# A two-stage recurrence on one core: three engines loop over 64 steps instead of 8, one gate semaphore is split by parity, and VectorE makes its next wait value at another place

## What is computed

```python
# stage 1, GRU over keys: x = keys @ Wx + b, then for each of 1024 steps
z = sigmoid(xz + (h @ Wh)_z);  r = sigmoid(xr + (h @ Wh)_r)
h = z * h + (1 - z) * relu(xh + r * (h @ Wh)_h)        # all h are kept as outs
# between: attn = softmax over time of outs . (queries @ W_att.T)
# stage 2, attention GRU over outs, 1024 steps more
r = sigmoid(xr + (h @ Wh)_r);  c = relu(xc + r * (h @ Wh)_c)
h = (1 - a) * h + a * c                                 # a = attn[b, t]
```

## Time and profile before

| | |
|---|---|
| median of 3 runs | 4424.12 us (4422.9 to 4429.71) |
| profiled execution | 4430.53 us |
| its span, first to last instruction | 4428.7 us |
| granted TensorE clock, mean | 0.997 |
| GRU loops | about 16 to 2316 us |
| attention loops | about 2353 to 4425 us |

### The profile page before, as it was taken

The page is one execution under the profiler, slowest core; times in us unless marked ns, Lnnn a source line. Parts: engine busy times, 40 slices in busy tenths (PEclk is TensorE's granted clock), DMA queues, the critical chain, the costliest instruction groups (busy, mean ns, idle before and its releaser), DMA issues.

```text
span 4428.7 us, 336421 instructions
## 1 busy us (share of the span) xinstructions
PE 4372.4 (99%) x131196; PEld 3968.0 (90%) x131196; DVE 4196.2 (95%) x24625; ACT 2286.8 (52%) x9363; POOL 2717.1 (61%) x6154
## 2 busy tenths in 40 slices
PE   8999999999999999999998999999999999999999
PEld 7888888888888888888887999999999999999998
DVE  8999999999999999999998999999999999999999
ACT  5666666666666666666654444444444444444444
POOL 6777777777777777777773444444444444444444
PEclk9999999999999999999998999999999999999999
DMA  3333333333333333334334555555555555554554
GB/s 110 115 116 123 115 116 123 115 115 121 117 115 120 119 115 120 119 115 121 118 123 129 129 132 128 128 132 128 128 133 128 128 133 128 128 133 129 127 133 115
DMA packets 169275, 544.13 MB, mean 123 GB/s; under 512 B 31644, under 2 KB 38060, under 8 KB 169260
## 3 DMA queue, kind: packets, MB, share of 16 engines
q1 hardware_dynamic: 169260, 543.93, 44.3%
HBM read 405.24 MB, written 138.56 MB: 123 GB/s over the span
## 4 chain that ended last, share of the span: by engine, by line
DVE 52%; PE 21%; issue 20%; DMA 3%; DVEq 2%; SPq 1%; ACT 0%; ACTq 0%; PEldq 0%
DVE vec_bank L525 12%; DVE gated L448 8%; DVE state L538 7%; DVE a_new L532 6%; DVE vec_bank L455 5%; DVE gated L519 5%; DVE vec_bank L464 5%; DVE h L475 4%; PE r_bank_a L561 4%; PE r_bank_b L561 3%; DMA logits<-logit_rows 2%; PE logit_bank L623 2%; PE z_bank_b L569 2%; PE z_bank_a L569 2%; PE c_bank_a L561 1%
## 5 line engine op out<-in xcount | busy, mean ns | idle before, releaser
L331 POOL TENSOR_TENSOR a_kept<-attn_rest,state 128x128 f32<-128x128 f32 x2048 | 933.6, 456 | 1173.6 <-DVE state L538 1139.0
L314 POOL TENSOR_TENSOR kept<-z_gate,h 128x128 f32<-128x128 f32 x2048 | 933.6, 456 | 533.8 <-ACT z_gate L360 512.0
L304 POOL TENSOR_TENSOR prod<-h,qw 128x128 f32<-128x128 f32 x2050 | 934.6, 456 | 0.0
L569 PE MATMUL r_bank_a<-x,weights 64*64 64x128 f32 x8200 | 881.7, 290 | 12.8 <-ACT r_gate L389 7.1
L569 PE MATMUL r_bank_b<-x,weights 64*64 64x128 f32 x8192 | 892.8, 295 | 0.0
L569 PE MATMUL z_bank_a<-x,weights 64*64 64x128 f32 x8200 | 853.9, 283 | 0.0
L569 PE MATMUL z_bank_b<-x,weights 64*64 64x128 f32 x8192 | 843.3, 283 | 0.0
L623 PE MATMUL logit_bank<-prod,row_sum 64*64 64x128 f32 x8208 | 798.5, 270 | 8.6 <-ACT logit_rows L349 5.0
L464 DVE SCALAR_TENSOR_TENSOR vec_bank<-vec_bank,z_rest 128x64 f32<-128x64 f32 x4096 | 735.9, 225 | 0.4 <-issue 0.3
L475 DVE TENSOR_TENSOR h<-vec_bank,kept 128x64 f32<-128x64 f32 x4096 | 721.3, 218 | 0.0
L389 ACT ACTIVATE r_gate<-r_bank_a 128x128 f32<-128x128 f32 x1024 | 284.0, 277 | 837.5 <-PE r_bank_a L561 837.5
(11 more groups left out here) (119 smaller groups left out, 17857.4 us busy)
## 6 DMA issues: line engine op xcount, KB each, us to landing
x<-in_keys_t SPq DMA_DIRECT2D x512, 256.0 KB, 3.7
gru_outputs<-h SPq DMA_DIRECT2D x256, 512.0 KB, 2.9
x<-gru_outputs SPq DMA_DIRECT2D x512, 256.0 KB, 3.7
attn<-attention SPq DMA_DIRECT2D x512, 256.0 KB, 3.9
logits<-logit_rows SPq DMA_DIRECT2D x258, 8.0 KB
time_rows<-logits SPq DMA_DIRECT2D x2, 896.0 KB, 7.0
attention<-time_rows SPq DMA_DIRECT2D x2, 896.0 KB, 5.5
weights<-in_weight_columns SPq DMA_DIRECT2D x2, 176.0 KB, 3.7
```

The lines of the kernel that those rows point to most:

```text
L304: nc.gpsimd.tensor_tensor(prod[:, (s - 1) % BODY, gcols(g)], h_at(s - 1)[:, gcols(g)], qw[:, gcols(g)], ALU.mult).then_inc(prod_ready[g], 1)
L314: nc.gpsimd.tensor_tensor(kept[:, g], z_gate[:, g], h_at(s - 1)[:, gcols(g)], ALU.mult).then_inc(kept_ready[g], 1)
L331: nc.gpsimd.tensor_tensor(a_kept[:, s % 2, gcols(g)], attn_rest[:, s % 2, gcols(g)], state[:, (s - 1) % 2, gcols(g)], ALU.mult).then_inc(a ...
L569: last = nc.tensor.matmul(dst[lanes(half)], weights[lanes(1 - half), w], moving[lanes(1 - half)], start=start, stop=False, skip_group_chec ...
```

## The change

VectorE, ScalarE and GpSimd loop over bodies of `SPAN = 64` written-out steps; TensorE and SP keep bodies of 8. `r_ready` and `ar_ready` become two semaphores each, for even and odd steps, off which TensorE takes 4 at the last two steps of its body; with them go the wait and the increment at a body's start. VectorE's `due` no longer is an expression but a register, filled one step ahead, behind the second group's candidate. Values that depended on `s` within 8 steps are taken `s % BODY`.

```diff
+SPAN = 8 * BODY
-        r_ready, z_ready, zr_ready = sems("r_ready"), sems("z_ready"), sems("z_rest_ready")
+        r_ready, ar_ready, anew_ready = parity_sems("r_ready"), parity_sems("ar_ready"), parity_sems("anew_ready")
+        def by_parity(s):
+            return s % BODY // 2 + 1
...
-            with act.Fori(0, T, BODY) as t0:       # the same on pool and dve, in both stages
-                for s in range(BODY):
-                    if s == 2:
-                        copy_logits(t0)
+            with act.Fori(0, T, SPAN) as t0:
+                for s in range(SPAN):
+                    if s % BODY == 2:
+                        copy_logits(t0 + (s - 2))
...
             def gru_gated(due, s, g):
-                if s == 0:
-                    dve.wait_ge(r_summed[g], due)
-                    dve.sem_inc(bodies_begun, 1)
                 dve.wait_ge(rh_summed[g], due)
-                dve.wait_ge(r_ready[g], s + 2)
+                dve.wait_ge(r_ready[g][s % 2], by_parity(s))
...
-                stored = t0 * ONES + 16
-                for s in range(BODY):
-                    due = t0 + (s + 2)
+                soon = count(0, t0, 2)              # reg_add into one of two registers
+                for s in range(SPAN):
+                    due = soon
+                    if s % CHUNK == 0:
+                        stored = t0 * ONES + 16 * (s // BODY + 1)
                     for g in GROUPS:
                         gru_gated(due, s, g)
                         gru_cand(due, s, g)
+                        if g == 1:
+                            soon = count(s + 1, t0, s + 3)
                         gru_new(due, s, g)
                         gru_h(due, stored, s, g)
...
             def agru_gated(due, s, g):
-                if s == 0:
-                    dve.wait_ge(ar_summed[g], due)
-                    dve.sem_inc(bodies_begun, 1)
-                dve.wait_ge(ar_ready[g], s + 2)
+                dve.wait_ge(ar_ready[g][s % 2], by_parity(s))
                 dve.wait_ge(rc_summed[g], due)
...
                     agru_cand(due, s, 1)
+                    soon = count(s + 1, t0, s + 3)
                     agru_new(due, pairs, s, 1)
...
-                        pe.wait_ge(r_ready[o], seen_by_pe(s, o))
+                        pe.wait_ge(r_ready[o][(n - 1) % 2], by_parity(n - 1))
-                        if n % BODY == 0:
-                            last.then_inc(ar_ready[o], -BODY)
+                        if (n - 1) % BODY >= BODY - 2:
+                            last.then_inc(ar_ready[o][(n - 1) % 2], -HALF)
```

More of the change, by code:

```diff
@@ L26, in recurrent_attention_kernel @@
     BM = HALVES * COLS // P
-    assert HALVES == 2 and GC == P and T % BODY == 0
+    assert HALVES == 2 and GC == P and T % SPAN == 0
     BODIES = T // BODY
@@ L56, in part_sems, with parity_sems @@
             return [[sem(f"{name}_{'ab'[g]}{part}") for part, _ in PARTS] for g in GROUPS]
+        def parity_sems(name):
+            return [[sem(f"{name}_{'ab'[g]}_{('even', 'odd')[parity]}") for parity in range(2)] for g in GROUPS]
         weights = sb("weights", [P, 11, U])
@@ L305, in product @@
                                         ALU.mult).then_inc(prod_ready[g], 1)
-            with pool.Fori(0, T, BODY) as t0:
-                for s in range(BODY):
+            with pool.Fori(0, T, SPAN) as t0:
+                for s in range(SPAN):
                     due = t0 + (s + 2)
@@ L338, in _ @@
                 act.sem_inc(zr_ready[g], FIRST)
-                for q in (r_ready[g], ar_ready[g]):
-                    act.sem_inc(q, (1, FIRST)[g])
+            act.sem_inc(r_ready[1][1], HALF)
+            act.sem_inc(ar_ready[1][1], HALF)
             act.sem_inc(rest_ready, 1)
@@ L349, in copy_logits @@
                 nc.scalar.activation(logit_rows[:], logit_bank[:, 0:COLS], ACT.Copy).then_inc(logits_copied, BODY)
-            with act.Fori(0, T, BODY) as t0:
-                for s in range(BODY):
-                    if s == 2:
-                        copy_logits(t0)
+            with act.Fori(0, T, SPAN) as t0:
+                for s in range(SPAN):
+                    if s % BODY == 2:
+                        copy_logits(t0 + (s - 2))
                     due = t0 + (s + 2)
@@ L460, in gru_new @@
                 for part, c in PARTS:
-                    dve.wait_ge(cand_ready[g][part], (due, s + 2)[part])
+                    dve.wait_ge(cand_ready[g][part], (due, s % BODY + 2)[part])
                     if part == 0:
-                        dve.wait_ge(zr_ready[g], s + 2)
+                        dve.wait_ge(zr_ready[g], s % BODY + 2)
                     nc.vector.scalar_tensor_tensor(new[:, c], cand[:, c], 0.0, z_rest[:, g, c],
@@ L473, in gru_h, with count @@
                         if g == 0 and s % CHUNK == 0:
-                            dve.wait_ge(outs_stored[s // CHUNK], stored)
+                            dve.wait_ge(outs_stored[s // CHUNK % 2], stored)
                     last = nc.vector.tensor_tensor(h_at(s)[:, gcols(g)][:, c], new[:, c], kept[:, g, c], ALU.add)
                 last.then_inc(h_ready[g], 1)
-            with dve.Fori(0, T, BODY) as t0:
-                stored = t0 * ONES + 16
-                for s in range(BODY):
-                    due = t0 + (s + 2)
+            counts = [dve.alloc_register(f"dve_count_{i}") for i in range(2)]
+            def count(i, base, more):
+                dve.reg_add(counts[i % 2], base, more)
+                return counts[i % 2]
+            with dve.Fori(0, T, SPAN) as t0:
+                soon = count(0, t0, 2)
+                for s in range(SPAN):
+                    due = soon
+                    if s % CHUNK == 0:
+                        stored = t0 * ONES + 16 * (s // BODY + 1)
                     for g in GROUPS:
@@ L539, in agru_sum @@
                                         a_kept[:, s % 2, gcols(g)], ALU.add).then_inc(s_ready[g], 1)
[L541 to L545, removed]
+            with dve.Fori(0, T, SPAN) as t0:
+                done, soon = t0 + 1, count(0, t0, 2)
+                for s in range(SPAN):
+                    due = soon
+                    if s % CHUNK == 0:
+                        pairs = t0 * PAIRS + 32 * (s // BODY + 1)
                     agru_gated(due, s, 0)
```

42 lines of the change are left out of this document (22 added, 20 removed).

## The result

The changed kernel takes 4543.4 us (median of 4 runs, 4542.2 to 4546.0) beside 4426.3 us: ratio 1.0265, 95% interval 1.0248 to 1.0283. It is slower by 117 us where 58 us of gain were forecast, and it lies above the range. Its profiled execution has a span of 4540.4 us against 4428.7 us.

The account below looks back on a forecast made before the run. VectorE's pace within steps and its idle at back edges were taken to bound the kernel. Terms -60 - 6 - 52 - 82 + 142 = -58 us took 4424.1 us to 4366 us, range 4275 to 4445.

Parts of the forecast that it names:

- Part 1, GRU: GRU loops: removed back edges save 0.47 x 128 = 60 us, plus 6 us of after-effect; remaining edges priced separately.
- The 0.25 us behind an edge: Extra time of the GRU steps behind a back edge, mean per body; 0.05 us of it counted as saved, 6 us.
- Part 1, attention: Attention loops: removed back edges save 0.41 x 128 = 52 us; the first step's extra 0.10 us stays.
- TensorE's own loops ... at nothing: TensorE keeps bodies of 8 steps; its split counts use as many waits and decrements, at no cost.
- Part 2: VectorE's `due` made behind the second group's candidate: attention stage saves 82 us (bounds 0 to 92), GRU stage 0.
- rival (4): GRU stage: the moved addition costs 0.03 us a step, 31 us in all, giving 4397 us; chance 0.06.
- rival (3): Attention stage: the moved addition gives nothing, as TensorE or `r_gate` is late next; 4448 us, chance 0.12.
- Part 3: Remaining back edges, 15 per loop: long bodies are refetched, 4.75 us an edge, 142 us in all (74 to 182).
- the term of the low clock: Clock falls as TensorE runs dry at a remaining back edge: 0.9 us added per edge, bounds 0 and 1.8.
- straight code is fetched ahead of use: Inside the long bodies, code is fetched before it is needed; no cost was entered for it.
- (1): No refetch: each remaining jump back costs 0.5 us as now, 30 times, giving 4239 us; chance 0.15.
- (2): Remaining back edges dearer than all bounds, deciding from 6.7 us an edge; at 7.0 us, 4434 us; chance 0.17.

Follow-up runs that it names:

- e4: Changed kernel with SP's store of the logits issued ahead of the second half's load and store instead of behind them: 4461.2 us, ratio 1.0078.
- e7: Kernel before the change, with the logits' store issued earlier and nothing else: 4420.2 us, ratio 0.9979.
- e11: Changed kernel with ScalarE and GpSimd back at bodies of 8 steps, VectorE alone at 64: 4541.9 us, ratio 1.0252.
- e5: Changed kernel with bodies of 8 steps and the logits' store issued earlier: 4312.9 us, ratio 0.9730.
- e9: e4 plus, in all six loops of the three engines, an instruction per pass that asks for the code behind the back edge ahead of the jump: 4346.8 us, ratio 0.9807.

## Why the prediction was wrong, step by step

The forecast was 177 us low. Its terms, by the table of steps, the loops and the experiments:

**Part 1, GRU: "60 us, and 6 us" for the removed edges, is the step that failed most.** The edges went, and a middle body without the logits' wait is 17.4 us, 0.08 us less than I had left. But the round trip of the logits' store then ends last at step 2 of each body: 80 us (after against e4). The 0.25 us behind an edge that I took for a start-up effect contained the beginning of it (10 us, e7). I named ScalarE's waits for that store as part of it and did not ask what happens to a wait of 39 us when its cover of 0.47 us per body is taken away; with the cover's row in hand the question was answerable. Net 70 us missed.

**Part 1, attention, and "TensorE's own loops ... at nothing".** The first step's 0.10 us stayed as said. But every eighth step still takes 0.26 us more, at TensorE's own back edge (by its place, as said), which VectorE's had hidden: 0.26 x 128 = 33 us missed.

**Part 2 held.** The value behind the candidate makes a step 1.87 us, 0.09 us less (92 us; the term was 82). GRU steps stayed at 2.155 us, so rival (4) fell, and the near tie with `r_gate` of rival (3) did not matter. This gives back 10 us of the miss.

**Part 3: the mechanism held, one size was a little low, and a term was lacking.** Bodies are fetched again, the edges wait, and the clock falls behind them. The Trainium skill (Runtime: NRT & Kernel Launch, "Instruction fetch mechanics") has it that a taken branch out of a small window waits for its code; the traces agree that such an edge waits. The window of 512 instructions that it names is not the length of a loop that stays, since passes of 324, 372 and 475 wait; whether the window is smaller, or the fetch ahead takes part of it, was not tried. An edge cost 4.05 to 4.1 us of spell and 1.25 to 1.4 us behind it, 5.4 us, against 4.75: 30 x 0.65 = 20 us, most of it in the term of the low clock, 0.9 where it is 1.3. It lies inside the bounds of 2.45 to 6.05. The code fetched for VectorE, 1.5 + 0.9 MB by the prediction, was 3.1 MB (e11's queue), with that of ScalarE and GpSimd on top. What had no term is the price of straight code: "straight code is fetched ahead of use" I took to mean at no cost. It pauses at each 128 instructions, (2.0 + 1.8) x 16 = 60 us. The same section of the Trainium skill puts the blocks at 256 instructions and calls their crossing "mostly hidden"; here the measurement decides, 128 instructions and up to 0.35 us each.

Together 70 + 33 - 10 + 20 + 60 = 173 of 177 us; 4 us are open. A check of the sizes by the loops of e4: bare steps would be 1024 x 2.155 = 2207 and 1024 x 1.873 = 1918 us, so its loops of 2333 and 2072 us hold 280 us more. The 30 edges (162), the short spells (60) and the pattern of the other 112 bodies of each loop (0.13 and 0.35 us each, 54) make 276. The same for e5, whose loops hold 2276 - 2207 + 1978 - 1918 = 129 us more, gives 0.54 and 0.47 us for each body of 8, its short edge included. Long bodies thus could have gained 0.54 - 0.13 = 0.41 and 0.12 us a body, 52 and 15 us in all, had nothing of part 3 come: less than the 118 of the forecast, since TensorE's edge and the start of a body stay.

**The rivals.** (1) was excluded by the packets. (2), dear edges, named the right side with half of the reason: an edge costs 5.4 us, under its point of 6.7. With the pauses of straight code, 60/30 = 2 us for each edge, it would be over it, and the logits come on top. The two losses that made the sign, the store's round trip and the pauses of straight code, stood in no rival.

## What to carry to other kernels

Before a stall is removed, list every wait that ended within its length of it, a DMA's round trip above all: the next to end last can be hidden there, as it was here, where moving one store's issue was worth 80 us and the removed edges, by the account above, 67. A loop body on an engine that sets the pace should stay small enough not to be fetched again (here 275 instructions stayed, 324 did not); above that, each pass pays for the jump and for its straight code. Make computed wait values where the engine has a dependent gap anyway.

## What the runs showed of the hardware that I had not expected

- Straight code on VectorE, where its body is fetched in each pass, pauses up to 0.35 us every 128 instructions, on the mean 0.17 us in the GRU stage (2.0 us for 11.6 a pass) and 0.24 us in the attention stage (1.8 us for 7.6), and does so with the fetch ahead of the edge too (e9).
- What stays on an engine is less than I thought: passes of 247 (VectorE) and 275 instructions (ScalarE) are not fetched again, 324 (GpSimd), 372 (VectorE) and 475 (ScalarE) are. In the changed kernel an engine whose pass is fetched again issues nothing behind the branch for 3.5 us on GpSimd, 3.9 on ScalarE, and 3.8 (GRU) or 4.25 (attention) on VectorE (medians); with bodies of 8 it was 0.1 to 0.3 us.
- Behind the spell of 4.2 us shown above the granted clock is 0.50, and the two steps behind an edge take 1.25 to 1.4 us more. The mean clock fell from 0.997 to 0.986.
- In e9 the jump with its start fetched ahead still costs 2.0 us in the GRU stage (the two steps around it take 2.84 and 3.60 us for 2.21 and 2.24) and 0.4 us in the attention stage (2.53 and 1.98 for 2.13 and 1.96). The granted clock stays at 1.00 there (medians). What differs is a further spell: in each of the 15 GRU passes behind an edge VectorE stands 1.0 to 1.6 us ahead of the 22nd instruction behind the branch, the place of the first short spell above. In the attention stage the first such place is the 47th instruction, and it has 0.2 us. That the short way to it is the reason was not tried.
